# Transposing the next batch's inputs by DMA instead of on TensorE, in a four-layer attention and adapter kernel

## What is computed

```python
# layer 0: 16 heads of 32; queries from f, keys and values from x, and f's own key as one more
q = (f + b_self) @ Wq + bq
k = concat([x + b_prev, f + b_self]) @ Wk + bk
v = concat([x, f]) @ Wv + bv
x = x + (softmax(mask(q k^T * SCALE), with the self score) applied to v) @ Wo + bo
# layer 1: one head over the whole width
x = x + softmax((x + bias[stage]) @ f^T) @ f
# layer 2: adapter with layer norm, weights picked by language
h = relu(x @ W1 + b1)
x = x + layernorm(x + h @ W2 + b2) * gamma + beta
# layer 3: low rank, weights picked by language
x = x + (x @ A^T) @ B^T * SCALING + emb
```

## Time and profile before

| | us |
|---|---|
| median of three runs | 1380.03 |
| the profiled execution | 1377.38 |
| its span in the trace | 1375.5 |
| PE busy | 1298.6 (94%) |
| DVE busy | 919.0 (67%) |
| ACT busy | 878.9 (64%) |
| POOL busy | 424.8 (31%) |

### The profile page before, as it was taken

The page is one execution under the profiler, slowest core; times in us unless marked ns, Lnnn a source line. Parts: engine busy times, 40 slices in busy tenths (PEclk is TensorE's granted clock), DMA queues, the critical chain, the costliest instruction groups (busy, mean ns, idle before and its releaser), DMA issues.

```text
span 1375.5 us, 20006 instructions
## 1 busy us (share of the span) xinstructions
PE 1298.6 (94%) x7049; PEld 562.8 (41%) x7049; DVE 919.0 (67%) x1600; ACT 878.9 (64%) x1857; POOL 424.8 (31%) x372
## 2 busy tenths in 40 slices
PE   6999999999999999999998999999999999999995
PEld 3332553325533355333543245432464425533252
DVE  4786459855697556974489645896458864598544
ACT  3798338873488645885468753698437883388731
POOL 3521054310732006520165103541045310543114
PEclk9999999999999999999999999999999999999997
DMA  5303022021122112130131301213013030220200
GB/s 177 85 24 103 15 56 70 27 92 32 46 62 80 39 31 63 47 114 4 31 78 39 110 1 44 69 36 110 1 55 75 27 102 14 58 69 24 64 1 31
DMA packets 62161, 75.82 MB, mean 55 GB/s; under 512 B 14378, under 2 KB 35174, under 8 KB 62062
## 3 DMA queue, kind: packets, MB, share of 16 engines
q1 hardware_dynamic: 62000, 74.53, 19.1%
q10 hardware_dynamic: 62, 0.01, 0.0%
HBM read 40.81 MB, written 8.40 MB: 36 GB/s over the span
## 4 chain that ended last, share of the span: by engine, by line
PE 74%; ACT 12%; DVE 10%; issue 2%; POOL 1%; DMA 0%; ACTq 0%; POOLq 0%
PE bank L461 29%; PE banks L461 12%; ACT big L798 7%; DVE nmx L1018 6%; PE bank L1365 6%; PE bank L1199 6%; PE banks L1349 6%; PE banks L1284 5%; ACT banks L747 4%; PE bank L1339 2%; PE bank L1312 2%; PE bank L1317 2%; PE bank L1375 1%; PE bank L1330 1%; DVE st L966 1%
## 5 line engine op out<-in xcount | busy, mean ns | idle before, releaser
L747 ACT ACTIVATE banks<-banks,nmx 128x512 f32<-128x512 f32 x512 | 342.5, 692 | 47.8 <-DVE nmx L1018 45.5
L1018 DVE TENSOR_REDUCE nmx<-banks 128x1 f32<-128x512 f32 x512 | 329.0, 686 | 36.6 <-PE banks L1284 36.4
L798 ACT ACTIVATE big<-banks 128x1024 f32<-128x1024 f32 x256 | 247.3, 1022 | 43.6 <-PE banks L1349 42.5
L461 PE MATMUL bank<-fT,w_hi 128*128 128x512 f16 x768 | 260.6, 384 | 0.1
L1284 PE MATMUL banks<-KQ 97*128 97x512 f16 x512 | 197.6, 386 | 30.6 <-ACT banks L747 28.8
L535 POOL TENSOR_TENSOR big<-x,b2r 128x512 f32<-128x512 f32 x32 | 40.5, 1266 | 383.1 <-DVE x L947 373.4
L1349 PE MATMUL banks<-KQ 98*128 98x512 f16 x512 | 141.0, 382 | 13.4 <-ACT big L798 8.4
L461 PE MATMUL bank<-fT,w_lo 128*128 128x512 f16 x384 | 147.1, 383 | 0.0
L496 POOL TENSOR_TENSOR half<-qk,ones 128x512 f16<-128x512 f32 x64 | 67.1, 1048 | 246.5 <-ACT qk L729 224.0
L1365 PE MATMUL bank<-big,V 128*32 128x512 f32 x1024 | 136.4, 605 | 0.0
L747 ACT ACTIVATION_READ_ACCUMULATOR banks<-banks,nmx 128x1 f32 x512 | 120.8, 236 | 0.0
(11 more groups left out here) (149 smaller groups left out, 1965.5 us busy)
## 6 DMA issues: line engine op xcount, KB each, us to landing
KQ<-half SPq DMA_DIRECT2D x384, 64.0 KB, 2.0
tiles_in<-in_x_dram SPq DMA_DIRECT2D x32, 256.0 KB, 7.0
tiles_in<-in_fside_BxSxS_dram SPq DMA_DIRECT2D x32, 256.0 KB, 2.8
x<-in_x_dram SPq DMA_DIRECT2D x8, 1024.0 KB, 5.8
out_dram<-x SPq DMA_DIRECT2D x32, 256.0 KB, 2.0
w<-in_L_cond_W_dram SPq DMA_DIRECT2D x16, 256.0 KB, 4.8
b2r<-in_L_cond_b_dram SPq DMA_DIRECT2D x8, 256.0 KB, 4.5
gr<-in_L_cond_gamma_dram SPq DMA_DIRECT2D x8, 256.0 KB, 5.5
```

Source lines behind the costliest of these rows:

```text
L461: mm = eng.matmul(out_ap, pairs[n][0], pairs[n][1], start=(first and n == 0), stop=(last and n == len(pairs) - 1))
L747: eng.activation(bank(step, i)[:, v, :], bank(step, i)[:, v, :], ACT.Exp, bias=nmx[:, t, h:h + 1], accum_out=esum[:, t, h:h + 1]).then_inc ...
L798: eng.activation(big[:, n % 2, 2 * u:2 * u + 2, :], bank(step)[:, :, :], ACT.Exp).then_inc(read(step), 1)
L1018: eng.tensor_reduce(nmx[:, t, h:h + 1], bank(step, i)[:, v, :], AX_X, ALU.max, negate=True).then_inc(max_done, 1)
```

## The change

The steps NIN and IN are gone for all batches but the first. In their place, POOL splits each x tile and each f tile of batch i + 1 into f16 halves in split16[b % 2], tile by tile, high and low side by side as [128, 1024], and SP turns each with one transposing DMA, SBUF to SBUF, into xT and fT, high and low half at once: eight DMAs of 256 KB a batch (`turn`). f's halves take the place of x's in split16, and remain there for PV1, so POOL's F16 splits are no longer steps of order_mid but part of this.

The order is: SP loads the x tiles as before; POOL splits them behind its bias additions (`split_x`); SP loads each f tile when the x tile is split (`load_f`). SP turns x when the last WO has read aT. POOL then waits for all four turns of x (xt_in), and splits f (`split_f`). SP turns f tile by tile when the last S1 has read fT. PE waits for xt_in at K(0) and for ft_in at Q(0).

Nothing is dealt into the lists where NIN and IN were. split16 is twice as large as f16 was; to make room, t1 and t2 are now the two rows of y, and self2 and shift lie in p1_both. The bank plan is written anew: it gives every step of every batch its bank and its count one by one.

The diff, cut to what matters here:

```diff
-    slots = [("IN", NT), ("IN", NT + 1), *parts(("K", 0))[:2], ("IN", NT + 2), *parts(("K", 0))[2:4],
-             ("IN", NT + 3), *parts(("K", 0))[4:]] + parts(("Q", 0)) + parts(("KS", 0))
+    slots = (parts(("K", 0)) if tail else [("IN", NT), ("IN", NT + 1), *parts(("K", 0))[:2], ("IN", NT + 2), *parts(("K", 0))[2:4],
+             ("IN", NT + 3), *parts(("K", 0))[4:]]) + parts(("Q", 0)) + parts(("KS", 0))
...
-        later[f16_at + 4 * n] = [("F16", n)]
+        later[f16_at + 4 * n] = [] if tail else [("F16", n)]
...
-ORDER_L1 = [("WOP", 1), ("WOP", 2), ("WO", 0), ("WO", 1), ("WOP", 3), ("X1T", 0), ("X1T", 1), ("WO", 2),
-            ("WO", 3), ("S1", 0), ("X1T", 2), ("S1", 1), ("X1T", 3), ("P1T", 0), ("S1", 2),
-            ("P1T", 1), ("PV1", 0), ("S1", 3), ("P1T", 2), ("PV1", 1), ("NIN", 0), ("P1T", 3), ("NIN", 1),
-            ("PV1", 2), ("NIN", 2), ("NIN", 3), ("PV1", 3)]
-NIN_BANKS = (3, 0, 3, 1)
...
+ORDER_L1 = ([("WOP", 1), ("WOP", 2), ("WO", 0), ("WO", 1), ("WOP", 3), ("X1T", 0), ("X1T", 1), ("WO", 2),
+             ("WO", 3), ("S1", 0), ("X1T", 2), ("S1", 1), ("X1T", 3), ("P1T", 0), ("S1", 2),
+             ("P1T", 1), ("PV1", 0), ("S1", 3), ("P1T", 2), ("PV1", 1), ("P1T", 3), ("PV1", 2), ("PV1", 3)])
...
-        f16 = sb("f16", [P, 2, NT, D], F16)
+        split16 = sb("split16", [P, 2, NT, 2, D], F16)
...
-        self2 = sb("self2", [H, 2, S])
...
-        t1 = sb("t1", [P, S])
-        t2 = sb("t2", [P, S])
...
+        t1, t2 = y[:, 0, :], y[:, 1, :]
...
+        self2 = p1_both[0:H, 0]
+        shift = p1_both[0:H, 1, 0, 0:S // 2].bitcast(F16)
...
+            def split_x(i):
+                b = i + 1
+                if i >= 1:
+                    wait_full(eng, ("PV1", NT - 1), i - 1)
+                for n in range(NT):
+                    eng.wait_ge(tile_in[n], b * 32 + 16)
+                    split(split16[:, b % 2, n, 0, :], split16[:, b % 2, n, 1, :], tiles_in[:, n, :],
+                          x_hi, i * NT + n + 1, x_lo)
+            def split_f(i):
+                b = i + 1
+                for n in range(NT):
+                    if n == 0:
+                        eng.wait_ge(xt_in, i * NT * 16 + NT * 16)
+                    eng.wait_ge(tile_in[n], b * 32 + 32)
+                    split(split16[:, b % 2, n, 0, :], split16[:, b % 2, n, 1, :], tiles_in[:, n, :],
+                          f_hi, b * NT + n + 1, f_lo)
...
+                split_x(i)
+                split_f(i)
...
-            def swap_tiles(i):
+            def load_f(i):
                 for n in range(NT):
-                    wait_full(eng, ("NIN", n), i)
+                    if i < 0:
+                        wait_full(eng, ("NIN", n), i)
+                    else:
+                        eng.wait_ge(x_lo, i * NT + n + 1)
                     load_tile(n + NT, i + 1)
+            def turn(big_t, n, b, landed):
+                eng.dma_start_transpose(big_t[:, :, :, n * P:(n + 1) * P].rearrange("p h d n -> p (h d) n"),
+                                        split16[:, b % 2, n, :, :].rearrange("p h n -> p (h n)")).then_inc(landed, 16)
+            def turn_tiles(i):
+                b = i + 1
+                wait_full(eng, ("WO", NT - 1), i)
+                for n in range(NT):
+                    eng.wait_ge(x_lo, i * NT + n + 1)
+                    turn(xT, n, b, xt_in)
+                wait_full(eng, ("S1", NT - 1), i)
+                for n in range(NT):
+                    eng.wait_ge(f_lo, b * NT + n + 1)
+                    turn(fT, n, b, ft_in)
...
-                swap_tiles(i)
+                load_f(i)
+                turn_tiles(i)
...
-                    if kind == "NIN" and head:
-                        take_high(step, i, xT)
-                    elif kind == "X1T":
+                    if kind == "X1T":
...
+                    if step == ("K", 0):
+                        if first:
+                            wait_read(eng, ("NIN", NT - 2), -1)
+                            wait_read(eng, ("NIN", NT - 1), -1)
+                        else:
+                            eng.wait_ge(xt_in, b * NT * 16)
                     if step == ("Q", 0):
-                        wait_read(eng, ("IN", 2 * NT - 2), b)
-                        wait_read(eng, ("IN", 2 * NT - 1), b)
+                        if first:
+                            wait_read(eng, ("IN", 2 * NT - 2), b)
+                            wait_read(eng, ("IN", 2 * NT - 1), b)
+                        else:
+                            eng.wait_ge(ft_in, b * NT * 16)
...
-                    if kind == "NIN" and head:
-                        next_x(step, i)
-                    elif kind == "WOP":
```

More of the change, by code:

```diff
@@ L54, with parts @@
 NROWS = LOW_ROW + H
+def parts(step):
+    return [("PART", n, step) for n in range(PARTS - 1)] + [step]
 def order_mid(tail, head):
@@ L180, in plan_banks @@
     for g in range(NG):
-        give(3, ("SELF", g))
+        home.update({("SELF", g): 3, ("NORMS", g): 2, ("SELFW", g): 3, ("PV", g): g % 2})
+        home.update({("ST", g, k, u): (4, 6)[u] for k in range(NT) for u in range(2)})
+    for t in range(NT):
+        home.update({("WO", t): (4, 6)[t // 2], ("X1T", t): t % 2, ("P1T", t): t % 2, ("S1", t): 2 + t % 2,
+                     ("PV1", t): (4, 6)[t % 2], ("NIN", t): (4, 6)[t % 2], ("IN", NT + t): 2 + t % 2})
+        home.update({(kind, t): 2 for kind in ("X2T", "HID", "ADP", "X3T", "LOW", "LORA")})
@@ L182, in plan_banks, with order_attention @@
+    return home
+def order_attention():
+    order = []
     for g in range(NG):
-        give(2, ("NORMS", g))
-        give(3, ("SELFW", g))
-        give(g % 2, ("PV", g))
         for k in range(NT):
-            give(4, ("ST", g, k, 0))
-            give(6, ("ST", g, k, 1))
-    give(2, ("PREPB",))
-    give(3, ("PREPA",))
-    ring = {"X1T": (0, 1), "P1T": (0, 1), "S1": (2, 3), "PV1": (4, 6), "NIN": NIN_BANKS}
-    for t in range(NT):
-        give((4, 6)[t // 2], ("WO", t))
-    for step in ORDER_L1:
-        if step[0] in ring:
-            give(ring[step[0]][step[1] % len(ring[step[0]])], step)
@@ L198, in plan_banks @@
-    for step in order_mid(True, False):
-        if step[0] not in ("NORM", "SCALE", "SQ"):
-            give(2, step)
-    where = {step: (k, c) for k, steps in uses.items() for c, step in enumerate(steps)}
-    return where, {k: len(steps) for k, steps in uses.items()}
-WHERE, USES = plan_banks()
+            order += [("ST", g, k, 0), ("ST", g, k, 1)]
+        order += [("PV", g), ("NORMS", g), ("SELFW", g)]
+    return order + [("PREPB",), ("PREPA",)]
 ADAPTER_BANKS = (2, 3, 0, 1)
@@ L212, in order_last @@
     cut = ORDER_L1.index(("PV1", 1)) + 1
-    return ([step for step in ORDER_L1[:cut]]
+    return (ORDER_L1[:cut]
             + [("X2T", 0), ("P1T", 3), ("HID", 0), ("X2T", 1), ("PV1", 2), ("ADP", 0), ("HID", 1), ("SQ", 0),
@@ L331, in build_program @@
         pair = {k: ctx.enter_context(nc.psum_tensor(f"banks{k}", [P, 2, 512], F32)) for k in (4, 6)}
-        full = {k: sem(f"full{k}") for k in USES}
-        free = {k: sem(f"free{k}") for k in USES}
+        full = {k: sem(f"full{k}") for k in (0, 1, 2, 3, 4, 6)}
+        free = {k: sem(f"free{k}") for k in (0, 1, 2, 3, 4, 6)}
         def place(step, b):
-            if isinstance(b, int) and b == B - 1 and step in LAST:
-                return LAST[step]
-            k, c = WHERE[step]
-            return k, b * USES[k] + (BEFORE[k] + c)
+            return WHERE[step, b] if (step, b) in WHERE else (HOME[step], None)
         def bank(step, b=0):
@@ L1209, in weigh_values @@
                 hi_lo(eng, tile_of(step, i), [(p1T[:, t % 2, 0, k, :], p1T[:, t % 2, 1, k, :]) for k in range(NT)],
[L1210 removed]
+                      [(split16[:, i % 2, k, 0, :], split16[:, i % 2, k, 1, :]) for k in range(NT)]).then_inc(done(step, i), 1)
             def project(step, part, b, first=False):
@@ L1238, in project @@
                     right = [(src[:, 0, d, :], src[:, 1, d, :]) for d in range(ND)]
-                return hi_lo(eng, bank(step)[:, :], left, right, part=part)
+                return hi_lo(eng, bank(step, b)[:, :], left, right, part=part)
             def mid(tail, head, i, order=None):
```

90 lines of the change are left out of this document (47 added, 43 removed).

## The result

The changed kernel takes 1333.74 us (median of 4, 1332.8 to 1336.0) against 1380.51 us, a ratio of 0.966 (95% interval 0.963 to 0.968): 46.8 us less, where 21 were forecast. Its profiled execution took 1336.03 us, with a span of 1334.2.

A forecast was written before the change was run, and what follows sets the result against it. PE was taken as the bound, gapless outside the score maxima. 1377.4 - 24.4 (transposes) + 3.5 (POOL beside DVE) = 1356.5 us, or 1359 us as a median; range 1343 to 1403, leaving D out.

The forecast's parts named there:

- What bounds the kernel: PE is gapless from 470 to 555 us, so a microsecond taken there is a microsecond of the end.
- what is removed: Eight NIN or IN transposing steps leave PE per batch, 3.48 us each batch, 24.4 us over seven.
- A: Rival: PE was not the bound at the transposes, which filled waits that now show; 1371 us, chance 0.04.
- E: Rival: the change does not do what it says and PE keeps its transposes; given no chance.
- The turns: Transposing DMAs of x and f: at 1.8 us each, fT at about 506.7 us, 3.3 early for Q(0).
- s: Pace of one 128x1024 transposing DMA, taken as 1.8 us; fT is in time up to 2.60 us.
- Rival C: fT comes late at Q(0), with s between 2.60 and 3.42 us: 1359 to 1405 us, chance 0.12.
- eight times s: Two serial rounds of four turns make fT ready at 489.2 + 8s, for s above 2.24 us.
- Rival D: A turn is paid per 128x128 block, s 5.1 us, PE waits 20 us at Q(0): 1511 us, chance 0.18.
- POOL beside DVE: POOL's f split over the second attention's softmax lengthens small DVE instructions: 0.5 us a batch, +3.5 us.
- Rival B: POOL holds DVE longer, 1.6 us a batch in place of 0.5: 1367 us, chance 0.06.
- What moves along: Adapter steps stand four slots later, re-dealing ACT, DVE and POOL in the score phase; taken as 0, 12 us in range.

The follow-up runs named there:

- the changed kernel with the old dealing: Changed kernel with four empty slots where the IN steps stood, so adapter steps are dealt as in the kernel before; 1354.3 us, ratio 0.981.
- the thrice-turned kernel: Changed kernel with each transposing DMA issued three times, dummies ahead of the real one; 1440.7 us, ratio 1.045.
- the dealing alone: Kernel before, transposes still on PE, with IN steps not counted when adapter steps are dealt; 1369.3 us, ratio 0.992.
- the splits alone: Kernel before without POOL's f16 splits in batches 1 to 7, PV1 using batch 0's halves; 1378.9 us, ratio 1.000.
- for both: Kernel before with adapters dealt as in the changed kernel and without POOL's f16 splits in batches 1 to 7; 1360.3 us, ratio 0.985.
- each turn twice: Changed kernel with a dummy turn of the same size and source ahead of every real one; 1353.5 us, ratio 0.981.

## Why the prediction was right, and where it was wrong

**What bounds the kernel, and what is removed: right.** A microsecond taken in the gapless stretch came out at the end. 3.48 us a batch were forecast, and the changed kernel with the old dealing has just 3.5 us a batch less than before. Rivals A and E are out.

**The turns: right.** s = 1.37 us lies between the bounds of 0.99 and 2.55, nearer the load than the copies that I leaned on with 1.8. Landing was 1.9 us behind the last issue for 2.0; but the 2.0 of the earlier trace rows counts from the start of a copy's issue, and by that measure a turn takes 3.3 us, so that the two agree in part by luck. fT was 5.1 us early for 3.3. Rival C is out at this pace, and its arithmetic was near: the thrice-turned kernel waits 12.4 us a batch for 11.8. Its "eight times s" holds only for turns that set the pace; at 1.37 us the turns of f waited for the last S1 (488.46), as the text allowed. Its "for smaller s it is sooner than that" is wrong: under 2.24 us POOL's splits set the pace, and fT comes at 485.0 + 4s + 8.95 + s + 2.0, which is later than 489.2 + 8s. It changes nothing here, for at s = 1.8 that is 505.0, and the term with the last S1 gives 506.7. In the chances, too, C stands with half of its 0.12 as faster, and the sum takes 0.04 of it.

**Rival D: wrong by a factor.** A turn is not paid block by block: 1.37 us for eight blocks is 0.17 us for one. The Trainium skill, "VectorE: DVE Perf Modes", The three transpose paths, has 1309 ns for one block of 128x128. The page's figure is for one block by itself, which no run here shows; as a price for each block of a larger turn it doesn't hold here. Rival D had 0.18, and nothing on record beforehand could settle it: no row showed a transposing DMA.

**POOL beside DVE: the size was wrong, 0 for 3.5 us, and it was priced from the wrong row.** POOL's f splits do run beside the softmax of layer 1, and L1174 and L1177 (L1143 and L1146 before) pay nothing. DVE:

```profile
482.01 0.14 DVE L1174 TENSOR_SCALAR rrec<-rsum 128x1 f32<-128x1 f32 x1
482.19 0.16 DVE L1177 RECIPROCAL rrec<-rrec 128x1 f32<-128x1 f32 x1
```

The first begins inside POOL's split of 481.10 to 482.14, and the second lies over the start of that of 482.22 to 483.39. In the whole trace of the changed kernel 21 of 32 L1174 and 17 of 32 L1177 start while POOL works, and all take 0.14 to 0.17 us. The 1.19 us of the earlier trace rows belong to an instruction on 128x2 elements, these are on 128x1; I took "small, on SBUF" for the kind. Rival B is out. The small price kept the miss small; it was a choice between bounds of 0 and 1.6 us, and not knowledge.

**What moves along: this step failed.** It was put at 0 "with half of it, 12 us, in the range", because "nothing tells the sign"; it measured 19.4 us (2.77 x 7). The idle time of PE at stake, 3.56 us a batch, was read rightly in the third hand-over the earlier trace rows; it was not seen that DVE, held by POOL, ended the longest part of it, nor that the clock behind it differs between hand-overs. A gain could have been looked for: behind the 2.48 us of idle PE stood ACT waiting for DVE's maxima, and DVE in three instructions of 1.16 to 1.19 us that take 0.17 elsewhere. The prediction had a row of the kind in hand and used it only for what the change might cost. That very row, at 523.57 us, would have misled: it is of row tiles 0 and 1, where freeing DVE by 5.2 us a batch gave nothing. Only the walk back from PE's wait finds the three that count. Two things then take POOL away from there. With the new dealing the HALF split and the beta additions are over when DVE comes to NORM(2, 0), and no longer beside it; and the f16 splits, which would have filled the gap, are gone from the score phase. The runs with the kernel before give 1.65 us a batch for the dealing alone, 0.1 for the splits alone, and 2.8 for both; about 0.3 us of it is the clock that no longer falls.

**The rest.** 1359 less 19.4 us and less the 3.5 us of POOL beside DVE is 1336, against 1333.7. In the range, 12 us stood for a term whose own bound was 25; with the bound its low end would have been 1330 and held the time.

## What to carry to other kernels

Before pricing a re-ordering at zero, follow the longest wait of the bounding engine back to the instruction that ends it, and compare that instruction's duration with its duration elsewhere: a 0.17 us instruction that takes 1.19 us there may be a gain, and names its neighbour. The walk back comes first: where it does not lead, the same lengthening, 5.2 us a batch of it, was worth nothing. Keep POOL idle, or its work elsewhere, while DVE does small two-column work on SBUF that the bounding engine waits for. And when one of two covers is taken away and nothing moves, the second still hides it: remove both before calling either free.

## What the runs showed of the hardware

**DVE and POOL.** In the traces of both kernels a DVE instruction waits for POOL's only if it works on SBUF alone and has more than one element a partition: TENSOR_SCALAR and TENSOR_TENSOR on st, 128x2, take 0.15 to 0.17 us with POOL idle and 0.3 to 1.21 beside it; those on 128x1 keep their 0.14 to 0.16 us, and those that read PSUM their 0.69 (L1170, L1121). It also holds for large ones: L1136 on SBUF takes 0.75 us with POOL idle and 1.4 to 1.5 beside the x splits in the attention phase, which PE doesn't feel (48.7 us before, and in six of the seven batches after). The Trainium skill, "SBUF — State Buffer", Who interferes with whom, has this as an exclusive lock: DVE instructions in a 2-port mode and GpSimd's shut each other out for a whole instruction, those with two SBUF inputs contend with a GpSimd instruction that reads SBUF, and others don't contend. The traces agree, in that the pieces end with POOL's instruction (L963 at 559.39, POOL's split at 559.37).

**Transposing DMAs.** 256 KB from SBUF to SBUF are issued every 1.37 us, one, two or three to a tile, and a turn takes 3.3 us from its issue to its landing (the median of all three runs). Behind the last issue of a set that is 1.8 to 1.9 us in 13 of the changed kernel's 14 sets and 3.3 in one; with each turn twice it was 2.8 to 3.0 us in three of the seven sets of x. While they run the 16 DMA engines are busy for 1.00 of the time, at 189 GB/s (529 to 540 us in the kernel with three turns). The Trainium skill, "DMA: Bandwidth & Descriptors", Latency and other measured facts, has 261 GB/s for a transposing DMA; here the measured 189 decides.

**The clock.** In the kernel with each turn twice, waits of PE of 0.80 to 1.89 us left the granted clock at 1.00, and those of 2.03, 2.12 and 3.08 us were followed by 0.66 over 5 us; so was one of 12.78 us in the kernel with three turns. The length of the wait alone doesn't decide it: of the seven waits of 2.26 us in the kernel before, four were followed by a lower clock and three were not.
